# Order of work around the cross-attention maxima in a software-pipelined transformer block

## The chip, the cores and the metric

One core of a Trainium2 chip runs the whole kernel. The metric is the device time of one execution in microseconds (us); lower is better. An execution is one launch of the program, with inputs and outputs in device memory.

## What is computed

32 independent samples of 128 tokens and 128 channels pass one transformer block with 16 heads of width 8: modulated self-attention, cross-attention to a context of 77 tokens, and an MLP with 512 hidden columns. Cut to what matters here:

```
x_norm = modulate(_ln(x), shift_a, scale_a)
q, k, v = split(x_norm @ W_qkv + b_qkv)
attn_out = softmax(q k^T * scale) v @ W_proj + b_proj        # 128 x 128 scores per head
x = x + gate_a * attn_out                                    # called x1 below
q_c = _ln(x) @ W_qc + b_qc
k_c, v_c = split(_ln(context) @ W_kvc + b_kvc)
c_attn_out = softmax(q_c k_c^T * scale) v_c @ W_cproj + b_cproj   # 128 x 77 scores per head
x = x + c_attn_out                                           # called x2 below
x = x + gate_m * (gelu(modulate(_ln(x), ...) @ W_mlp1 + b_mlp1) @ W_mlp2 + b_mlp2)
```

## The kernel before, in words

The 32 samples are worked in 16 pairs. The five engines each run their own instruction stream, written out by hand, and meet through semaphores; every engine takes its stream in order. The attention part is a software pipeline: time is cut into slots, and a slot into 8 beats (t = 0 to 7). In one slot several pairs are at work at once, each in a different phase: `a` (the pair ahead: layer norm and q, k, v), `h` (here: maxima of the self scores, and their exponentials), `d` (one back: end of self-attention, the residual that makes x1, its layer norm, q of the cross-attention, k and v of the context), `f` (two back: the maxima of the cross scores), `e` (three back: cross exponentials and values) and `z` (four back: cross projection and second residual). Slots run from -2 to 19. Slots 0 to 15 have a pair `h`; slots 16 to 19 drain the pipeline and have none. Slot 16 still has `d`, `f`, `e` and `z`; slot 17 has `f`, `e` and `z`. The MLP over 8 groups of 4 samples follows, and its first steps are laid into slots 17 and 18: the first up-projection (`m_up`, L1168) stands at the head of slot 18 on the tensor engine and waits for all maxima of the cross scores.

A softmax needs each row's maximum ahead of the exponential. The tensor engine computes a unit of scores row-wise (`scores`, L1107) into `ps_max`; the vector engine reduces it (`maxima`, L740: `mx` for self, `mxc` for cross). A pair has 4 units u0 to u3, two for each sample. When a sample's two units are done, the pool engine (GpSimd) splits its maxima into two bf16 parts (`split_max`, L565 and L567: `nm`, `nmc`), the tensor engine transposes them (`max_t`, L1222; the job is called max_c0 for the first sample of a cross pair, max_c1 for the second), the scalar engine copies them out (L913) and SyncE's DMA queue writes them as extra rows into the stacked operands (L412). Only then can the transposed scores (`scores_t`, L1118) and the exponentials (L900) of that sample run. The stacked operands themselves (`qk_st`, `qkc_st`) are built by six DMAs for each pair (L407) from parts that the pool engine splits off (`parts`, `high`, `low`; L534, L536, L546, L548). Values are multiplied at L1129. A ring makes units of self and cross scores share `ps_max` in order.

Self units stand in beats 0 to 3, cross units in beats 4 to 7. The small jobs of a beat follow the unit on the tensor engine: the projection (`proj`, L1338 and L1341) in beat 4, k and v of the context (`kv_c`, L1350 and L1354) in beat 5; max_c0, the flipped cross sums (`oc_t`, L1204) and the transposed x1 (`x1_t`, L1196) in beat 6; the q projection of the cross-attention (`q_c`, L1217) and the flipped cross output (`obc_t`, L1204) in beat 7. On the vector engine the residual that makes x1 stands in beat 4 (L757), statistics and their aggregation in beat 5 (L702, L709), the normalisation in beat 6 (L718, writes `x_n`), the division of the cross output (`attention_out`, L747 and L751) at the head of beat 7. The pool engine turns the variance into the reciprocal deviation (`rstd`, L524 and L529). In the trace a digit in a name is left out: x_mv, x_ve, x_rstd and x_n stand for x and for x1 alike; SPq is SyncE's queue of DMA issues.

Of the kernel before, what the change touches and what calls it, by code (L numbers as in the profile page):

```python
# [26 lines left out]
S = 77  # L27
# [156 lines left out]
def block_kernel(nc, x, cond, ctx, w_mod, b_mod, w_qkv, b_qkv, w_proj, b_proj, w_qc, b_qc, w_kvc, b_kvc,  # L184
# [5 lines left out]
    with es:  # L190
# [303 lines left out]
        def _(pool):  # L494
# [65 lines left out]
            def split_max(p, b, mxt, nmt, counted, high, both, taken):  # L560

                if not p.first():
                    w(pool, taken, 2 * p.n + b - 1)
                hold(pool, counted, NU * p.n + 2 * b + 2)
                nc.gpsimd.tensor_copy(nmt[:, b, 0], mxt[:, b]).then_inc(sems[high], 1)  # L565
                w(pool, high, 2 * p.n + b + 1)
                nc.gpsimd.tensor_tensor(nmt[:, b, 1], mxt[:, b], nmt[:, b, 0], ALU.subtract).then_inc(sems[both], 1)  # L567
# [17 lines left out]
            def slot(s):  # L585
                far, a, h, d, f = (s.pair(n) for n in ("far", "ahead", "here", "back1", "back2"))
                if f:
                    parts(f, qcx[:], [qkcp[:, 0, n] for n in range(3)], qcr[:], "qc0_set", "qc", "qkc_in")
                if s.last(2):
                    m_rstd_step(0)  # L590
                if far:
                    rstd("x", far)
                if h:
                    split_max(h, 0, mx, nm, "mx_set", "nmh_set", "nm_set", "mts_ps")
                if d:
                    gated(d)
                if a:
                    high(a, qkx[:], [qkp[:, :, n] for n in range(3)], qkr[:], "qkx_set", "qk", "qk_in")
                if h:
                    split_max(h, 1, mx, nm, "mx_set", "nmh_set", "nm_set", "mts_ps")  # L600
                if a:
                    low(a, [qkp[:, :, n] for n in range(3)], qkr[:], "qk")
                if d:
                    rstd("x1", d)
                if f:
                    split_max(f, 0, mxc, nmc, "mxc_set", "nmch_set", "nmc_set", "mtc_ps")
                if h:
                    rstd("ctx", h)
                if d:
                    parts(d, kcx[:].rearrange("c (b k) -> c b k", b=G), key_parts,  # L610
                          kcr[:].rearrange("c (b k) -> c b k", b=G), "kvc0_set", "kc", "qkc_in")
                if f:
                    split_max(f, 1, mxc, nmc, "mxc_set", "nmch_set", "nmc_set", "mtc_ps")
                if far and far.first():
                    pool.wait_ge(sems["x_n_set"], 1)
                    for par in range(2):
                        nc.gpsimd.memset(qkc_st[par][:, :, 1].bitcast(u32), 0).then_inc(sems["z_pool"], 1)
                    nc.gpsimd.memset(qkcp[:].bitcast(u32), 0).then_inc(sems["pad_set"], 1)
                    pool.wait_ge(sems["z_pool"], 8)
                    for par in range(2):  # L620
                        nc.gpsimd.memset(qkc_st[par][:, :, 1].rearrange("c m (b k) -> c m b k", b=G)[:, :, :, 0:S],
                                         1.0).then_inc(sems["zk_set"], 1)
                if a and a.first():
                    pool.wait_ge(sems["wc_in"], 16 * 2)
                    for n, src in ((2, wqc_sb), (3, wkvc_sb)):
                        for s_ in range(2):
                            last = nc.gpsimd.tensor_copy(
                                wdh[:, n, HALF * s_:HALF * (s_ + 1)].rearrange("c (d m) -> c d m", d=D),
                                src[:, 0:C].rearrange("c (m s d) -> c s d m", s=2, d=D)[:, s_])
                        last.then_inc(sems["wdc_set"], 1)  # L630
# [8 lines left out]
        def _(dve):  # L639
# [72 lines left out]
            def normalise(kind, p, src, taken):  # L712
                L = ln[kind]
                w(dve, f"{kind}_rstd_set", p.n + 1)
                if not p.first():
                    w(dve, taken, p.n)
                for b in range(G):
                    last = nc.vector.tensor_scalar(L["xn"][:, b], src(b), L["mv"][:, b, 0:1], L["rstd"][:, b:b + 1],  # L718
                                                   ALU.subtract, ALU.mult)
                last.then_inc(sems[f"{kind}_n_set"], 1)  # L720
# [7 lines left out]
            def x_of(p):  # L728
                return lambda b: xs[:, batch(p, b)].rearrange("t o c -> t (o c)")
# [63 lines left out]
            def slot(s):  # L793
                far, a, h, d, f, e, z = (s.pair(n) for n in ("far", "ahead", "here", "back1", "back2", "back3", "back4"))
                for t in range(BEATS):

                    if t == 3 and s.last(2):
                        dve.wait_ge(sems["x2_set"], NPAIR - 3)
                        m_norm(0, 0, True)
                    if t == 0 and s.last(1):  # L800
                        m_norm(1, 1)

                    if t == 1 and z:
                        residual(z, "projc_ps", "proj_c", "x2_set")
                    if t == 3 and d:
                        attention_out(d, "s", "o_t", "ot_ps", "rden_set", "o_set", "obt_ps")
                    if t == 7 and e:
                        attention_out(e, "c", "oc_t", "oct_ps", "rdenc_set", "oc_set", "obct_ps")

                    use = s.unit(self_max(t))  # L810
                    if use:
                        maxima(*use, "smax_ps", mx, T, "mx_set", "nm_set")
                    use = s.unit(cross_max(t))
                    if use:
                        maxima(*use, "smaxc_ps", mxc, S, "mxc_set", "nmc_set")

                    if t == 0 and far:
                        arrived("x_in", far, {0: (0,), 1: (1,), 4: (2,), 5: (3, 4)})
                        stats("x", far, x_of(far))
                        aggregate("x", far)  # L820
                        if far.first():
                            tables(range(2), 1)
                            head_columns()
                    if t == 4 and d:
                        residual(d, "proj_ps", "proj", "x1_set")
                    if t == 5 and d:
                        hold(dve, "x1_set", d.n + 1)
                        stats("x1", d, x_of(d))
                        aggregate("x1", d)
                    if t == 1 and h:  # L830
                        arrived("c_in", h, {0: (0,), 1: (1,), 3: (2, 3, 4)})
                        stats("ctx", h, ctx_of(h))
                        aggregate("ctx", h)
                    if t == 5 and far:
                        normalise("x", far, x_of(far), "xt_ps")
                        if far.first():
                            tables(range(2, 6), 2)
                            for st in qkc_st:
                                nc.vector.memset(st[:, :, 0].bitcast(u32), 0).then_inc(sems["zq_set"], 1)
                            for vt in v_m:  # L840
                                nc.vector.memset(vt[:], 0.0).then_inc(sems["z_dve"], 1)
                            key_sums()
                    if t == 6 and d:
                        normalise("x1", d, x_of(d), "x1t_ps")
                    if t == 7 and h:
                        normalise("ctx", h, ctx_of(h), "ctxt_ps")
                if a and a.first():
                    gate_rows()
# [230 lines left out]
        def _(pe):  # L1079
# [107 lines left out]
            def slot(s):  # L1187
# [37 lines left out]
                for t in range(BEATS):  # L1225
                    use = s.unit(self_max(t))
                    if use:
# [2 lines left out]
                        if u == 0:  # L1230
                            w(pe, f"qk_in{p.par}", 16 * NCMB * (p.turn + 1))
                        scores(p, u, qk_st, T, "smax_ps")
                    use = s.unit(cross_max(t))
                    if use:
                        p, u = use
                        ring_free(s, MAX_RING, "cross", u, max_read)
                        if u == 0:
                            w(pe, f"qkc_in{p.par}", 16 * NCMB * (p.turn + 1))
                        scores(p, u, qkc_st, S, "smaxc_ps")
                    use = s.unit(self_exp(t))  # L1240
                    if use:
                        p, u = use
# [123 lines left out]
                        flip_out("obc_t", "c", e, "oc_set", "obct_ps")  # L1366
                    if t == 7 and far:
                        transposed("x_t", "x", far, T, "xt_ps")
                    if h and h.first() and t < 4:
                        spread(4 + t, ps_st[:, t % 2])  # L1370
                if a and a.first():
# [60 lines left out]
```

## Time and profile before

| | us |
|---|---|
| median of 3 runs | 414.25 |
| lowest and highest | 413.67, 418.06 |
| the profiled execution's own time | 416.58 |
| its span, first to last instruction | 414.8 |
| mean granted TensorE clock in it | 0.960 |

The 1.78 us between the profiled execution's time and its span lie outside the instructions. Stretches of the trace are named by us from the start of the span. The self maxima of slot 0 begin at 26.1, of slot 3 at 80.1, of slot 11 at 218.8 and of slot 15 at 286.9; slot 16 begins at 303.4, and the first up-projection of the MLP starts at 336.9.

### The profile page before, as it was taken

What the parts mean: (1) busy time and instruction counts of PE and PEld (TensorE: products, weight loads), DVE (VectorE), ACT (ScalarE), POOL (GpSimd) and SP (SyncE); (2) the same over time, 40 slices, a digit from 0 to 9 for tenths busy, and PEclk for the clock granted to TensorE, in tenths of its full rate; (3) what the DMA queues carried; (4) which work ended last, traced back from release to release, by engine and by line L of the source; (5) the groups of instructions that cost most, each with busy time, mean ns of one, the idle gap of its engine ahead of it and who ended that gap; (6) DMA issues with size and microseconds to landing.
All of it is one profiled execution on the core that took longest, in us unless ns stands there. A gap on an engine that the chain in (4) does not pass through costs nothing.

```text
span 414.8 us, 15984 instructions
## 1 busy us (share of the span) xinstructions
PE 349.4 (84%) x5880; PEld 237.8 (57%) x5880; DVE 254.0 (61%) x650; ACT 268.6 (65%) x523; POOL 216.7 (52%) x494
## 2 busy tenths in 40 slices
PE   3475867889899989999899989998777787999994
PEld 2343545566666766767667667676555454445442
DVE  5653637668777887878877788777635350434311
ACT  1134444668677887878878887787672457577572
POOL 7724357657776676776867668666252310211200
PEclk9999978899999999999999999999997588999998
DMA  5053358251432424325343352343230300000101
GB/s 149 13 138 86 88 155 175 72 143 44 119 91 70 117 70 122 91 70 127 72 106 91 78 136 70 92 100 74 68 80 1 81 4 1 25 27 25 51 25 51
DMA packets 65548, 33.13 MB, mean 80 GB/s; under 512 B 8359, under 2 KB 65255, under 8 KB 65511
## 3 DMA queue, kind: packets, MB, share of 16 engines
q1 hardware_dynamic: 63599, 32.56, 32.1%
q8 instruction: 24, 0.39, 0.4%
q10 hardware_dynamic: 1912, 0.07, 0.3%
q14 instruction: 13, 0.11, 0.1%
HBM read 4.83 MB, written 2.10 MB: 17 GB/s over the span
## 4 chain that ended last, share of the span: by engine, by line
PE 37%; issue 20%; DVE 18%; POOL 11%; SPq 6%; DMA 3%; ACT 2%; ACTq 1%; DVEq 1%; POOLq 1%
DVE mx L740 10%; PE ps_o L1176 7%; PE wide L1168 7%; PE ps_o L1129 5%; SPq L407 5%; PE wide L1107 4%; POOL qkp L536 3%; PE ps_misc L1204 3%; PE ps_misc L1217 3%; PE wide L1118 3%; POOL qkp L534 2%; DMA qk_st<-nmT 2%; PE ps_misc L1196 2%; DVE x_stats L702 1%; DVE ctx_stats L702 1%
## 5 line engine op out<-in xcount | busy, mean ns | idle before, releaser
L740 DVE TENSOR_REDUCE mx<-wide 128x8 f32<-128x1024 f32 x64 | 78.0, 1219 | 27.1 <-PE wide L1107 27.1
L900 ACT ACTIVATE p_c<-wide 128x1024 f32<-128x1024 f32 x64 | 65.5, 1023 | 33.4 <-PE wide L1118 33.0
L900 ACT ACTIVATE p_s<-wide 128x1024 f32<-128x1024 f32 x64 | 65.5, 1024 | 21.5 <-PE wide L1118 21.0
L740 DVE TENSOR_REDUCE mxc<-wide 128x8 f32<-128x616 f32 x64 | 50.8, 794 | 24.7 <-PE wide L1107 24.6
L1129 PE MATMUL ps_o<-p_s,v_m 128*32 128x128 f32 x1024 | 44.5, 294 | 0.6
L1129 PE MATMUL ps_o<-p_c,vc_m 128*32 128x128 f32 x1024 | 44.3, 294 | 0.3 <-ACT s_sum L921 0.2
L524 POOL TENSOR_TENSOR x_ve<-x_mv,eps_sb 128x2 f32<-128x2 f32 x32 | 6.4, 201 | 57.9 <-DVE x_mv L709 57.9
L1118 PE MATMUL wide<-qk_st 64*128 64x128 bf16 x512 | 26.9, 226 | 7.6 <-DMA qk_st<-nmT 5.6
L1107 PE MATMUL wide<-qk_st 62*128 62x128 bf16 x512 | 27.3, 231 | 6.0 <-DVE mx L740 4.5
L1129 PEld LDWEIGHTS ps_o<-p_s,v_m 128*32 128x32 f32 x1024 | 26.1, 114 | 8.7 <-issue 3.5
L1129 PEld LDWEIGHTS ps_o<-p_c,vc_m 128*32 128x32 f32 x1024 | 25.7, 114 | 8.0 <-issue 1.1
L1168 PE MATMUL wide<-m_nT,w_sb 128*128 128x512 f32 x64 | 29.9, 602 | 0.2 <-DVE mxc L740 0.2
L1118 PE MATMUL wide<-qkc_st 64*128 64x128 bf16 x512 | 26.2, 223 | 3.5 <-ACT p_c L900 3.3
L1176 PE MATMUL ps_o<-qk_st,w_sb 128*128 128x512 f32 x64 | 28.9, 594 | 0.0
L1107 PEld LDWEIGHTS wide<-qk_st 62*128 62x128 bf16 x512 | 15.5, 99 | 23.1 <-DVE mx L740 18.7
L1107 PE MATMUL wide<-qkc_st 62*128 62x77 bf16 x512 | 20.5, 203 | 9.7 <-DMA qkc_st<-qkcp 9.3
L571 POOL TENSOR_TENSOR m_ve<-m_mv,eps_sb 128x4 f32<-128x4 f32 x8 | 1.6, 200 | 48.1 <-DVE m_mv L776 48.1
L1107 PEld LDWEIGHTS wide<-qkc_st 62*128 62x128 bf16 x512 | 12.3, 97 | 22.0 <-issue 18.7
L757 DVE TENSOR_TENSOR xs<-xs,ps_misc 128x256 f32 (+1 forms) x32 | 13.5, 421 | 18.3 <-PE ps_misc L1341 11.0
L529 POOL TENSOR_TENSOR x_rstd<-x_ve,mhalf 128x2 f32<-128x2 f32 x32 | 22.4, 700 | 2.9 <-POOL x_ve L524 0.8
L951 ACT ACTIVATE m_y<-ps_o,gb_m,mod 128x128 f32<-128x128 f32 x32 | 12.0, 456 | 18.0 <-PE ps_o L1176 18.0
L790 DVE TENSOR_TENSOR m_out<-xs,ps_misc 128x512 f32<-128x512 f32 x8 | 5.5, 687 | 29.6 <-PE ps_misc L1184 29.6
(154 smaller groups left out, 828.1 us busy)
## 6 DMA issues: line engine op xcount, KB each, us to landing
qk_st<-qkp SPq DMA_DIRECT2D x96, 128.0 KB, 2.6
qkc_st<-qkcp SPq DMA_DIRECT2D x96, 128.0 KB, 2.5
out<-m_out SPq DMA_DIRECT2D x8, 256.0 KB, 2.3
xs<-x SPq DMA_DIRECT2D x3, 512.0 KB, 3.9
qk_st<-nmT SPq DMA_DIRECT2D x64, 4.0 KB
qkc_st<-nmcT SPq DMA_DIRECT2D x64, 4.0 KB
ctx_sb<-ctx SPq DMA_DIRECT2D x3, 308.0 KB
w_sb<-L_xcond_W_mlp SPq DMA_DIRECT2D x2, 256.0 KB, 3.9
```

The lines of the kernel that those rows point to most:

```text
L407: sp.dma_start(dst[c:128:ROWSTEP], parts[:].rearrange("c a p t -> c (a p) t")[:, a:b + 4:b + 3 - a]).then_inc(sems[name], 16)
L529: nc.gpsimd.tensor_tensor(L["rstd"][:], L["ve"][:], mhalf[0:L["rows"], 0:G], ALU.pow).then_inc(sems[f"{kind}_rstd_set"], 1)
L536: nc.gpsimd.tensor_tensor(dst[2], rest, dst[1], ALU.subtract).then_inc(sems[f"{name}2_set"], 1)
L740: nc.vector.reduce_max(mxt[:, b].rearrange("q (x r) -> q r x", r=2)[:, r], src, AX.X, negate=True).then_inc(sems[done], 1)
L757: nc.vector.tensor_tensor(xs[:, batches(p)], xs[:, batches(p)], ps_misc[BANK[job]][:, 0:GT].rearrange("t (b c) -> t b c", b=G), ALU.add).t ...
L900: nc.scalar.activation(dst[u % 2][:].rearrange("k x q -> k (x q)"), ps_st[:].rearrange("k s x -> k (s x)"), ACT.Exp, scale=SCALE).then_inc ...
L1107: last = mm(ps_max[:, s_, j * T:j * T + keys], st[p.par][lo:lo + KROWS, m, 0, b * T:(b + 1) * T], st[p.par][lo:lo + KROWS, m, 1, b * T:b * ...
L1118: last = mm(ps_st[:, s_, j * T:(j + 1) * T], st[p.par][lo:lo + HALF, m, 1, b * T:(b + 1) * T], st[p.par][lo:lo + HALF, m, 0, b * T:(b + 1) ...
L1129: last = mm(ps_o[32 * j:32 * j + 32, at:at + T], vt[p.par][:, b, 4 * j + 2 * r + s_], probs[u % 2][:, 4 * s_ + j], start=(s_ == 0), stop=( ...
L1168: mm(ps_h[k], w1_sb[:, k * 128:(k + 1) * 128], m_nT[par][:], start=True, stop=True).then_inc(sems["m_h_ps"], 1)
L1176: last = mm(ps_y[:, :], w2_sb[:, k], hT[par][:, k], start=(k == 0), stop=(k == NF - 1))
L1204: last = tr(dst[:, n * 128:(n + 1) * 128], src, ident[:])
```

## The change

Three orders change; no instruction is added or taken away.

1. Pool engine, slots with `h`: `split_max(f, 0)` now comes ahead of `rstd("x1", d)`. It has an effect where `d` and `f` exist, in slots 2 to 15.
2. Vector engine, slots without `h` (16 and 17): the maxima of a cross unit come after the residual, the statistics and the normalisation of their beat, and the statistics of x1 move from beat 5 to beat 4. The division of the cross output stays ahead of the maxima in beat 7.
3. Tensor engine, slots without `h`: the row-wise cross scores come last in their beat, after the transposed scores, the values and the small jobs.

```
@@ pool, slot(s)
-                if d:
+                if d and not h:
                     rstd("x1", d)
                 if f:
                     split_max(f, 0, mxc, nmc, "mxc_set", "nmch_set", "nmc_set", "mtc_ps")
+                if d and h:
+                    rstd("x1", d)
@@ vector, slot(s), in the loop over t
                     use = s.unit(cross_max(t))
-                    if use:
+                    if use and h:
                         maxima(*use, "smaxc_ps", mxc, S, "mxc_set", "nmc_set")
...
-                    if t == 5 and d:
+                    if t == (5 if h else 4) and d:
                         hold(dve, "x1_set", d.n + 1)
                         stats("x1", d, x_of(d))
                         aggregate("x1", d)
...
                     if t == 6 and d:
                         normalise("x1", d, x_of(d), "x1t_ps")
+                    if use and not h:
+                        maxima(*use, "smaxc_ps", mxc, S, "mxc_set", "nmc_set")
@@ tensor, slot(s), in the loop over t
-                    use = s.unit(cross_max(t))
-                    if use:
-                        p, u = use
-                        ring_free(s, MAX_RING, "cross", u, max_read)
-                        if u == 0:
-                            w(pe, f"qkc_in{p.par}", 16 * NCMB * (p.turn + 1))
-                        scores(p, u, qkc_st, S, "smaxc_ps")
+                    def rows_max():
+                        ...
+                    if h:
+                        rows_max()
...
                     if t == 7 and far:
                         transposed("x_t", "x", far, T, "xt_ps")
+                    if not h:
+                        rows_max()
```

## Rows read from the trace of the kernel before

**Rows 1.** The page: busy time of each engine.

```profile
PE 349.4 (84%) x5880; PEld 237.8 (57%) x5880; DVE 254.0 (61%) x650; ACT 268.6 (65%) x523; POOL 216.7 (52%) x494
```

**Rows 2.** Timeline of PE, slot 10: start, duration, operands, [idle before <- releaser].

```profile
214.88 0.23 PE L1222 MATMUL ps_misc<-ident,nmc 128*32 128x128 bf16 x1 [0.80 <-POOL nmc L567]
215.53 0.38 PE L1196 MATMUL ps_misc<-ident,x_n 128*128 128x128 f32 x2
215.84 0.31 PE L1107 MATMUL wide<-qkc_st 62*128 62x77 bf16 x8
216.23 0.40 PE L1118 MATMUL wide<-qk_st 64*128 64x128 bf16 x8
```

**Rows 3.** Timelines of POOL and DVE, the same slot.

```profile
213.37 0.21 POOL L524 TENSOR_TENSOR x_ve<-x_mv,eps_sb 128x2 f32<-128x2 f32 x1 [1.69 <-DVE x_mv L709]
214.59 0.23 POOL L567 TENSOR_TENSOR nmc<-mxc,nmc 128x16 bf16<-128x16 f32 x1
...
211.71 0.79 DVE L740 TENSOR_REDUCE mxc<-wide 128x8 f32<-128x616 f32 x1
214.41 0.59 DVE L718 TENSOR_SCALAR x_n<-xs,x_mv,x_rstd 128x128 f32 x2
```

**Rows 4.** Timeline of SyncE's DMA issues, the same slot.

```profile
213.86 1.15 SPq L412 DMA_DIRECT2D qk_st<-nmT  x2
```

**Rows 5.** The chain that ended last, in order of time, slot 14.

```profile
282.88 1.63 DMA qk_st<-nmT
...
284.65 0.40 PE wide L1118 x8
```

**Rows 6.** Timelines of PE and of SyncE's issues, slot 3.

```profile
95.52 0.38 PE L1196 MATMUL ps_misc<-ident,x_n 128*128 128x128 f32 x2
95.84 0.32 PE L1107 MATMUL wide<-qkc_st 62*128 62x77 bf16 x8
95.99 0.39 PE L1118 MATMUL wide<-qk_st 64*128 64x128 bf16 x8
...
92.07 1.14 SPq L412 DMA_DIRECT2D qk_st<-nmT  x2
```

**Rows 7.** Timelines of PE, DVE and SyncE's issues, slot 15.

```profile
301.18 0.38 PE L1196 MATMUL ps_misc<-ident,x_n 128*128 128x128 f32 x2
...
299.97 0.60 DVE L718 TENSOR_SCALAR x_n<-xs,x_mv,x_rstd 128x128 f32<-128x128 f32 x2 [0.25 <-POOL x_rstd L529]
...
293.21 4.79 SPq L412 DMA_DIRECT2D qk_st<-nmT  x4
```

**Rows 8.** Timelines of PE and POOL, slot 16.

```profile
312.71 0.32 PE L1107 MATMUL wide<-qkc_st 62*128 62x77 bf16 x8 [2.75 <-DMA qkc_st<-qkcp]
318.63 0.22 PE L1222 MATMUL ps_misc<-ident,nmc 128*32 128x128 bf16 x1 [0.94 <-POOL nmc L567]
320.56 1.22 PE L1217 MATMUL ps_misc<-x1T,wdh 128*128 128x256 f32 x2 [0.38 <-ACT nmcT L913]
...
322.44 0.40 POOL L546 CAST qkcp<-qcx 128x256 bf16<-128x256 f32 x1 [0.73 <-issue]
```

**Rows 9.** Timelines of PE and DVE, slot 17 and the head of 18.

```profile
329.93 0.44 PE L1107 MATMUL wide<-qkc_st 62*128 62x77 bf16 x8 [0.85 <-DMA qkc_st<-qkcp]
332.12 1.08 PE L1129 MATMUL ps_o<-p_c,vc_m 128*32 128x128 f32 x16
333.13 1.12 PE L1158 MATMUL ps_misc<-ident,m_n 128*128 128x128 f32 x4
336.93 1.12 PE L1168 MATMUL wide<-m_nT,w_sb 128*128 128x512 f32 x2 [0.20 <-DVE mxc L740]
...
335.74 0.42 DVE L751 TENSOR_TENSOR c_o<-ps_misc,c_rden 128x256 f32<-128x256 f32 x1
```

**Rows 10.** Stretches of 6 us: engines' busy time, TensorE clock (PEclk), DMA.

```profile
312.00:318.00 6.00, 4.98 (x108) 3.79 (x108) 2.88 (x8) 2.12 (x4) 0.86 (x3) 0.72 0.00 0
...
324.00:330.00 6.00, 3.88 (x63) 2.28 (x62) 2.69 (x13) 3.07 (x3) 2.04 (x4) 0.50 0.55 133
```

More of the change, by code:

```diff
@@ L1232, in slot @@
                         scores(p, u, qk_st, T, "smax_ps")
-                    use = s.unit(cross_max(t))
-                    if use:
-                        p, u = use
-                        ring_free(s, MAX_RING, "cross", u, max_read)
-                        if u == 0:
-                            w(pe, f"qkc_in{p.par}", 16 * NCMB * (p.turn + 1))
-                        scores(p, u, qkc_st, S, "smaxc_ps")
+                    def rows_max():
+                        use = s.unit(cross_max(t))
+                        if use:
+                            p, u = use
+                            ring_free(s, MAX_RING, "cross", u, max_read)
+                            if u == 0:
+                                w(pe, f"qkc_in{p.par}", 16 * NCMB * (p.turn + 1))
+                            scores(p, u, qkc_st, S, "smaxc_ps")
+                    if h:
+                        rows_max()
                     use = s.unit(self_exp(t))
```

## The prediction, as recorded before the changed kernel was seen

> **What bounds the kernel now.** The page first: PE is the busiest engine at 84%, the others lie between 52% and 65% [rows 1]. That is too little for a bound by work alone, so the question is which waits lie on the path. I read three stretches: a slot of the loop, the two slots where a wait differs from the loop's, and the drain. Each is read on the timeline of PE first, then on the engine that released it.
>
> In a slot of the loop PE has one visible stall: 0.80 us ahead of max_c0, released by POOL's nmc [rows 2]. POOL had been idle 1.69 us, waiting for the mean and variance of x1, while the maxima that it was to split next were ready at 211.71 + 0.79 = 212.50 [rows 3]. The first edit goes for exactly this stall. But 1 us later PE meets a second gate that is easy to miss, for it stands between two groups that look adjacent. The row-wise cross scores start at 215.84 and the transposed self scores of unit 2 at 216.23, 0.39 us apart [rows 2]; in slot 3 the same two groups are 95.99 - 95.84 = 0.15 us apart [rows 6]. The missing 0.24 us are a wait for the DMA that writes the second sample's self maxima: it is issued as a pair at 213.86 and 1.15 us long [rows 4], and the chain of slot 14 shows that the second of a pair lands 1.63 us after its own start and PE starts 0.14 us after that [rows 5]. So 213.86 + 0.59 (half of the pair and the gap) + 1.63 + 0.14 = 216.22, and PE started at 216.23. In the timelines the distance from this pair's issue to those scores is 2.35 to 2.38 us in slot 2 and in slots 4 to 14, 12 slots with the same number: PE waits for the DMA in all of them.
>
> **Part 1, the split ahead of the deviation (slots 2 to 15).** POOL splits in its idle time: two instructions of about 0.2 us, 0.5 us with their gap, from 212.6 to 213.1. The mean and variance arrive for the instruction at 213.37 [rows 3], so the deviation isn't pushed back. Max_c0 leaves the path: it can run at about 213.9, when the values ahead of it are issued. What is late next is x1_t: it needs x_n, which ends at 214.41 + 0.59 = 215.00 [rows 3], and so starts at 215.05 to 215.15 where it now starts at 215.53 [rows 2]. At best that is 0.4 us for PE. Then comes the gate. The DMA pair hangs on POOL's parts of q and k and on the five stack DMAs that stand ahead of it in SyncE's queue and are issued back to back, all of it ahead of the edit and fed by the self maxima of beats 0 to 3, which follow the slot's start on PE. None of it moves. PE will wait about 0.6 us at the transposed scores where it now waits 0.24, and everything after them, the q projection and the next slot's first rows included, stays where it is. Gain in 12 slots: 0. Also moved are POOL's deviation of the context, the parts of the context's k and the first max DMA of the cross pair, each about 0.4 us earlier; nobody on the path waits for them.
>
> In two slots the gate is open. In slot 3 the pair was issued at 92.07 and landed by 92.07 + 0.59 + 1.63 = 94.3, while the scores ran at 95.99 [rows 6]; x1_t goes from 95.52 to about 95.1: 0.4 us, and slot 4 begins that much earlier with all that feeds its DMAs. In slot 15 the last of four issues ends at 293.21 + 4.79 = 298.00 and has landed by 299.1, long before x1_t at 301.18; x_n ends at 299.97 + 0.60 = 300.57 [rows 7], so x1_t can start at 300.7: 0.45 us. The lower bound of part 1 is therefore -0.85 us for both, the upper is 0 if either is eaten by a later DMA.
>
> **Part 2, slot 16.** PE stands 2.75 us at the cross rows of unit 0, for a DMA [rows 8], and behind this wait are queued the transposed scores of unit 3, the values and the projection. With the new order these run inside the stall: x1 is summed about 3 us earlier and its statistics are done at about 312.6. But the loop through the maxima is long. From the DMA (312.71 less the 0.4 won in slot 15, 312.3): rows 0.3, values and kv_c 2.2 (1.4 at full clock), rows 0.3, maxima 0.8, split 0.6, max_c0, oc_t and x1_t 1.3 to 1.7, copy 0.4. That puts q_c at 317.7 to 318.9 where it is 320.56 now [rows 8]. This gain isn't passed on whole. POOL's stream has the split of the second sample ahead of the parts of q_c; it waits for the maxima of unit 3, whose rows now stand on PE behind q_c and obc_t; obc_t waits for the division on DVE, and that stands behind the maxima of unit 2. So from x1_t: rows 0.3, maxima 0.8, division 0.9, obc_t 0.35, rows 0.3, maxima 0.8, split 0.5 = 4 us, a chain that now overlaps with q_c. POOL's first part of q_c, at 322.44 now [rows 8], comes at 321.2 (clock full) to 322.8 (clock halved). PEclk was 0.72 in this stretch [rows 10]; I take 321.8, 0.6 us earlier, the 0.45 of slot 15 in it.
>
> **Part 2, slot 17.** Its rows of unit 0 wait for the DMA that follows from POOL's parts, so they come 0.6 us earlier too. From them to the first up-projection it is now 336.93 - 329.93 = 7.0 us [rows 9], because the row scores run ahead of the jobs. In the new order each unit stands behind its beat's jobs: rows 0.4, values 1.1, m_transpose 1.1, rows 0.35, maxima 0.8, split 0.6, max_c0 and oc_t 0.8, rows 0.35, maxima 0.85, division 0.9, obc_t 0.35, rows 0.35, maxima 0.85 = 8.8 to 8.9 us. (Values, m_transpose and division by [rows 9], maxima and split by [rows 3].) What is moved ahead of the DMA (one unit of scores and of values) was off this chain before, too, once the ring of maxima is counted. So slot 17 costs 1.9 us, and no cover hides it: the up-projection is queued on PE ahead of max_c1, the projection and the last four exponentials, and DVE's next normalisation stands behind the same maxima.
>
> **Sum.** Slot 3 -0.4, slots 15 and 16 -0.6, slot 17 +1.9: +0.9 us. On the profiled execution's own time 416.58 + 0.9 = 417.5. That execution was 2.3 us over the median, so I put the sum on the median: 414.25 + 0.9 = 415.1. The runs shown spread by 4.4 us, which alone is 1%; a change of under 1%, 4.1 us, is what this kernel's times can't well tell from none.
>
> **Rivals.**
>
> A. The clock. After the 2.75 us stall PEclk is 0.72 from 312 to 318, and 0.50 from 324 to 330 [rows 10], against a mean of 0.96 over the span: at half clock 16 value products take 1.08 us [rows 9], where they take 0.64 in the loop. The new order breaks the long stall into pieces of 1 to 1.5 us. If the clock then stays full through slots 16 and 17, q_c's chain gives 1.9 us instead of 0.6, and slot 17's two groups on PE (2.2 us) halve nearly, while exponentials no longer wait for values at half clock: -0.4 - 1.9 + 1.9 - 1.2 = -1.6 to -2, 412.5 us. For it: the idle time is better spread. Against: the waits on POOL and DVE are new stalls of their own, and with the clock at 0.50 PE was busy 3.88 of 6 us.
>
> The Trainium skill speaks for this rival: "TensorE: Matmul & The Clock Gate" (HAM oscillation — how this bites in real kernels) says that long idle waits of the engine cost it the full clock and that tighter work keeps it. The trace agrees as to the fall after the stall at 312; whether shorter stalls are harmless no row shows.
>
> B. Part 1 is worth its 0.4 us in every slot, because the DMA pair moves with the rest: 14 x 0.4 = 5.6 less and 0.2 less in slot 16, 1.9 more in slot 17: 414.25 - 3.9 = 410.4 us. Against it stands the same 2.36 us in 12 slots.
>
> C. Slower: the new order of slots 16 and 17 lets PE idle more often, the clock falls earlier and comes back later than 334. Then slot 16 gives nothing (+0.4), slot 17 costs 2.3, and slot 18 runs at half clock: its four groups of values and two first up-projections cost 0.44 us more each (1.08 against 0.64), 2.6 us. 414.25 - 0.4 + 0.4 + 2.3 + 2.6 = 419.2 us. It decides if q_c comes later than 321.
>
> D. The reordering of slots 16 and 17 does nothing, as what is won ahead of the DMA is what is lost behind it: 413.4 to 414.3 us.
>
> **Chances.** Forecast (414.3 to 417.5) 0.50, D 0.15, A 0.17, B 0.07, C 0.08, the rest 0.03. The range of 8 in 10 takes in the forecast, D and most of A, and the spread of the runs: 411.8 to 417.8. Faster by over 1% (under 410.1) 0.07; slower by over 1% (over 418.4) 0.08; within 0.85.
>
> **What would show it.** Right: max_c0 has no idle time ahead of it in slots 2 to 15; x1_t starts 0.4 us sooner against the transposed scores of unit 2, which still start 2.36 us after the issue of the DMA pair; the slots of the loop still take 17.0 us. In slot 16 the projection runs ahead of the DMA's landing; in slot 17 the distance from rows u0 to the up-projection is near 9 us. Wrong: slots of 16.7 us in the loop (B), or PEclk of 1.00 from 318 to 330 (A). The forecast fails if the DMA pair's issue hangs on something that the early split also frees, or if the drain's clock differs from that of before.

## The result and the profile after

| | before, beside it | after |
|---|---|---|
| median of 4 runs, us | 416.15 | 420.41 |
| lowest and highest | 413.67, 418.13 | 419.17, 422.58 |
| the profiled execution's own time | 416.58 | 419.17 |
| its span | 414.8 | 417.4 |
| mean granted TensorE clock in it | 0.960 | 0.957 |

After over before is 1.0111 (interval 1.0066 to 1.0156): slower by 1.1%. The forecast was 415.1, range 411.8 to 417.8, with 0.85 on "within 1%". All ratios here and below leave out, as a slower state, executions that took over 1.5% longer than the fastest of their kernel; medians take in all.

Three places of the changed kernel answer to the rows of before. First a loop slot, in the timelines of PE, of SyncE's issues, of POOL and of DVE, the slot of [rows 2] to [rows 4]:

```profile
213.03 0.22 PE L1226 MATMUL ps_misc<-ident,nmc 128*32 128x128 bf16 x1
...
214.31 0.41 PE L1200 MATMUL ps_misc<-ident,x_n 128*128 128x128 f32 x2 [0.48 <-DVE x_n L720]
214.66 0.31 PE L1111 MATMUL wide<-qkc_st 62*128 62x77 bf16 x8
215.24 0.40 PE L1122 MATMUL wide<-qk_st 64*128 64x128 bf16 x8 [0.27 <-DMA qk_st<-nmT]
...
212.88 1.14 SPq L412 DMA_DIRECT2D qk_st<-nmT  x2
...
212.11 0.22 POOL L567 TENSOR_TENSOR nmc<-mxc,nmc 128x16 bf16<-128x16 f32 x1
212.54 0.21 POOL L524 TENSOR_TENSOR x_ve<-x_mv,eps_sb 128x2 f32<-128x2 f32 x1 [0.21 <-DVE x_mv L711]
...
200.71 1.22 DVE L742 TENSOR_REDUCE mx<-wide 128x8 f32<-128x1024 f32 x1 [1.20 <-PE wide L1111]
217.77 1.23 DVE L742 TENSOR_REDUCE mx<-wide 128x8 f32<-128x1024 f32 x1 [1.26 <-PE wide L1111]
```

Max_c0 no longer waits (of slots 2 to 15 only in slot 14, 0.32 us). X1_t now has the visible stall, 0.48 us, and the transposed scores have the other one, which this time the trace names: 0.27 us, for the DMA of the pair. They start 215.24 - 212.88 = 2.36 us after the issue of the pair, as before (216.23 - 213.86 = 2.37, [rows 2, 4]). The slot takes 217.77 - 200.71 = 17.06 us; the mean of the four slots 10 to 13 is 17.0 in both kernels. One wait went, the gate behind it stood, and the loop gained nothing.

Second, the drain on PE, and POOL's part of q_c; these answer to [rows 8] and [rows 9]:

```profile
311.12 0.32 PE L1111 MATMUL wide<-qkc_st 62*128 62x77 bf16 x8 [0.92 <-DMA qkc_st<-qkcp]
314.61 0.22 PE L1226 MATMUL ps_misc<-ident,nmc 128*32 128x128 bf16 x1 [1.67 <-POOL nmc L567]
316.25 0.70 PE L1221 MATMUL ps_misc<-x1T,wdh 128*128 128x256 f32 x2 [0.37 <-ACT nmcT L917]
...
327.50 1.08 PE L1133 MATMUL ps_o<-p_c,vc_m 128*32 128x128 f32 x16
328.51 0.44 PE L1111 MATMUL wide<-qkc_st 62*128 62x77 bf16 x8
...
332.76 0.22 PE L1226 MATMUL ps_misc<-ident,nmc 128*32 128x128 bf16 x1 [1.66 <-POOL nmc L567]
335.62 0.66 PE L1208 MATMUL ps_misc<-ident,c_o 128*128 128x128 f32 x2 [1.81 <-DVE c_o L753]
337.58 2.07 PE L1172 MATMUL wide<-m_nT,w_sb 128*128 128x512 f32 x2 [0.92 <-DVE mxc L742]
...
320.19 0.40 POOL L546 CAST qkcp<-qcx 128x256 bf16<-128x256 f32 x1
```

The 2.75 us stall of slot 16 is 0.92 now, though 1.67 us for POOL's split have come behind it, and q_c comes at 316.25 instead of 320.56. In slot 17 PE has three long waits: 1.66, 1.81 and 0.92 us, for POOL's split, for DVE's division and for the last maxima. Before, max_c0 had none there, and the last maxima cost 0.20 [rows 9]. The division cost 0.58:

```profile
334.42 0.23 PE L1222 MATMUL ps_misc<-ident,nmc 128*32 128x128 bf16 x1
...
336.32 0.41 PE L1204 MATMUL ps_misc<-ident,c_o 128*128 128x128 f32 x2 [0.58 <-DVE c_o L751]
```

From its first rows to the first up-projection it is 337.58 - 328.51 = 9.1 us, where it was 7.0 [rows 9]. The up-projection's line has a second message in its duration: its first two matmuls take 2.07 us where the same two took 1.12 [rows 9]. They are the same instructions at half clock. Third, therefore, stretches of after (us, then busy time of PE, PEld, DVE, ACT, POOL, then PEclk, DMA):

```profile
312.00:318.00 6.00, 3.23 (x49) 2.09 (x39) 3.21 (x7) 2.25 (x6) 2.65 (x8) 0.91 0.02 3
...
330.00:337.00 7.00, 3.19 (x35) 2.04 (x35) 2.56 (x5) 2.75 (x7) 0.41 (x2) 0.74 0.01 1
337.00:346.00 9.00, 7.25 (x85) 3.55 (x85) 3.25 (x14) 4.31 (x8) 1.62 (x4) 0.79 0.01 4
...
330.50:334.00 3.50, 1.66 (x24) 0.99 (x22) 0.91 (x2) 1.90 (x6) 0.41 (x2) 0.99 0.00 0
334.00:340.80 6.80, 4.25 (x33) 1.96 (x33) 3.76 (x14) 0.65 (x2) 1.62 (x4) 0.50 0.01 2
```

and of before, for 330 to 337 and 337 to 346, which the prediction does not show:

```profile
330.00:337.00 7.00, 6.04 (x84) 3.86 (x84) 3.93 (x8) 3.49 (x8) 0.41 (x2) 0.71 0.01 2
337.00:346.00 9.00, 7.27 (x109) 3.80 (x109) 2.59 (x13) 5.90 (x10) 1.62 (x4) 0.91 0.02 5
```

From 330 to 337 PE is busy 3.19 of 7 us, where it was 6.04. Before, the half clock of the drain ends in that stretch and slot 18 begins at full clock. After, the clock is full again already at 330.5, PE is busy 1.66 of the next 3.5 us, with the first of the three waits among them, and from 334.0 to 340.8 the clock is at half. So slot 18 begins at half clock, and from 337 to 346 PE runs 85 matmuls where it ran 109.

In what follows three distances of each profile stand beside the times: the period of a loop slot (a quarter of the time from the first self maxima of slot 10 to those of slot 14), slot 17 (from DVE's first cross maxima of the slot to the first up-projection), and the tail (from there to the end of the span). Before: 16.99, 6.51, 77.85. After: 17.00, 8.56, 79.79. So slot 17 is 2.05 us longer and what follows 1.94. Each distance is that of one profiled execution.

### The profile page after: what moved, and what is told of

The parts are those of the page before. It is cut to its first block and busy times, and to the rows that moved or that the text cites. A ratio compares the mean times of both kernels' runs of the same rounds, so it can differ in the third digit from the quotient of the medians.

```text
span 417.4 us, 15984 instructions
## 1 busy us (share of the span) xinstructions
PE 349.0 (84%) x5880; PEld 236.4 (57%) x5880; DVE 254.7 (61%) x650; ACT 269.1 (64%) x523; POOL 216.8 (52%) x494
## 5 line engine op out<-in xcount | busy, mean ns | idle before, releaser
L1133 PE MATMUL ps_o<-p_c,vc_m 128*32 128x128 f32 x1024 | 43.4, 290 | 0.8 <-ACT p_c L904 0.6
L1172 PE MATMUL wide<-m_nT,w_sb 128*128 128x512 f32 x64 | 31.5, 629 | 0.9 <-DVE mxc L742 0.9
L1122 PEld LDWEIGHTS wide<-qk_st 64*128 64x128 bf16 x512 | 17.2, 99 | 15.1 <-issue 12.0
L565 POOL CAST nmc<-mxc 128x16 bf16<-128x16 f32 x32 | 6.3, 195 | 35.4 <-issue 23.6
L1200 PE MATMUL ps_misc<-ident,x_n 128*128 128x128 f32 x64 | 14.0, 304 | 11.9 <-DVE x_n L720 11.8
```

Of the source, the lines that this page charges most:

```text
L1122: last = mm(ps_st[:, s_, j * T:(j + 1) * T], st[p.par][lo:lo + HALF, m, 1, b * T:(b + 1) * T], st[p.par][lo:lo + HALF, m, 0, b * T:(b + 1) ...
L1133: last = mm(ps_o[32 * j:32 * j + 32, at:at + T], vt[p.par][:, b, 4 * j + 2 * r + s_], probs[u % 2][:, 4 * s_ + j], start=(s_ == 0), stop=( ...
L1172: mm(ps_h[k], w1_sb[:, k * 128:(k + 1) * 128], m_nT[par][:], start=True, stop=True).then_inc(sems["m_h_ps"], 1)
L1200: last = tr(dst[:, b * rows:(b + 1) * rows], ln[kind]["xn"][:, b], ident[0:rows, 0:rows])
```

## The experiments

Ratios are to the kernel before, side by side, with the 95% interval, from 6 or 12 runs of the kernel and 23 or 29 of before. The medians of before beside them were 416.28 (e1 to e4), 417.26 (e5 to e8), 416.51 (e9 to e12) and 416.52 (e13 to e16).

**Which part costs: e1 to e4.** e1 has the pool engine's order alone; e2 has the new order of DVE and PE in slots 16 and 17 alone; e3 that in slot 16 alone, e4 in slot 17 alone.

```
 e1:  POOL hunk of the change only
 e2:  DVE and PE hunks only (POOL as before)
 e3:  -if use and h:        +if use and not s.last(3):     # s.last(3): slot 16
      -if not h: rows_max() +if s.last(3): rows_max()      # and so on, POOL as before
 e4:  the same with s.last(2)                              # slot 17
```

> Part 1 alone: only the pool engine's order changes, in slots 2 to 15. Gate theory (the DMA pair of the second sample's self maxima holds the transposed scores of unit 2 in 12 slots): the loop keeps its 17.0 us for a slot, max_c0 loses its stall, the distance from the pair's issue to those scores stays 2.36 us, and the whole is 0.5 to 1.5 us faster than before (what the trace of the changed kernel already shows up to slot 15: self maxima of slot 15 at 285.4 instead of 286.9). Rival (the early split itself costs time in executions that weren't profiled): 1 to 4 us slower. Rival (the gain adds up in every slot): 4 us or more faster.

> Parts 2 and 3 alone: the vector and tensor engines' order in slots 16 and 17, the pool engine's as before. If the drain is where the loss comes from: slower than before by what the whole change costs and what part 1 gives, 4 to 6 us, with rows u0 of slot 17 to the first up-projection at 9 us instead of 7.0. If the loss comes from the split: within 1 us of before.

> Only slot 16 has the new order on the vector and tensor engines; slot 17 and the pool engine are as before. Theory: slot 16 gains about 1 us (the pool engine's parts of the q projection come 1 us earlier, as in the changed kernel) and nothing in slot 17 gives it back: 0.5 to 1.5 us faster than before. Rival (both slots' orders are bad, because each breaks the tensor engine's work into more stalls and the clock falls): slower by 1 to 3 us.

> Only slot 17 has the new order. Theory: its chain from the rows of unit 0 to the first up-projection takes 9 us instead of 7.0, +2 us, and the first up-projection and slot 18 run at half clock for a further 1 to 2 us: 3 to 5 us slower than before. Rival (slot 17's loss is hidden by other work of slot 18): under 1 us.

| | ratio | median | slot | slot 17 | tail |
|---|---|---|---|---|---|
| e1 | 0.9995 (0.9962 to 1.0029) | 416.25 | 17.00 | 6.50 | 77.86 |
| e2 | 1.0109 (1.0071 to 1.0146) | 419.60 | 17.00 | 8.22 | 80.21 |
| e3 | 1.0004 (0.9963 to 1.0045) | 415.74 | 16.99 | 6.06 | 77.67 |
| e4 | 1.0106 (1.0054 to 1.0158) | 420.53 | 16.99 | 8.28 | 80.17 |

The whole loss is slot 17's. The split and slot 16, each expected to gain 0.5 to 1.5 us by itself, are worth nothing that can be measured. PE in e4 (timeline):

```profile
332.88 0.22 PE L1224 MATMUL ps_misc<-ident,nmc 128*32 128x128 bf16 x1 [1.67 <-POOL nmc L567]
...
335.97 0.66 PE L1206 MATMUL ps_misc<-ident,c_o 128*128 128x128 f32 x2 [1.81 <-DVE c_o L751]
...
337.93 2.08 PE L1170 MATMUL wide<-m_nT,w_sb 128*128 128x512 f32 x2 [0.92 <-DVE mxc L740]
```

The same three waits and the same up-projection at half clock as in the changed kernel, without the other two parts.

**Whether the DMA pair is the loop's gate: e5 and e6.** e5 moves the issue of the pair ahead of the last two of the five stack DMAs; e6 adds the split of part 1. If the pair is the gate, the slot gets shorter now, and the split, worth nothing by itself, gets a value.

```
 if a: w qk1_set; stack(..., 1)
+if h: w nmT_set; max_rows(qk_st[h.par], 1, nmT, ...)
 if a: w qk2_set; stack(..., 2)
-if h: w nmT_set; max_rows(qk_st[h.par], 1, nmT, ...)
```

> The kernel before, with one edit on SyncE's queue: the DMA pair of the second sample's self maxima is issued after three of the five stack DMAs instead of after all five. Gate theory: the pair can go when the scalar engine has copied the maxima out, about 1.3 us earlier, and no longer holds the transposed scores of unit 2; the stall at max_c0 is then the only one, and PE gains the 0.24 us that it now waits at those scores: 0.2 us in each of 12 slots, 2 to 3 us in all. Rival (the slot is set by the vector engine or by PE and the wait is incidental): no change, or up to 1 us slower since two stack DMAs go 1.2 us later.

> The same edit of SyncE's queue together with part 1, the early split. Gate theory: with the gate open the 0.4 us that the early split wins on PE before x1_t reach the next slot: 0.24 + 0.4 = 0.6 us in each of 12 to 13 slots, 7 us or 1.8% faster than before, slots of 16.4 us instead of 17.0. Rival (another gate stands right behind, such as the vector engine's chain of self maxima or the stack DMAs of the next pair): no more than the run without the split gives.

| | ratio | median | slot | slot 17 | tail |
|---|---|---|---|---|---|
| e5 | 0.9946 (0.9912 to 0.9981) | 414.18 | 16.80 | 6.55 | 77.84 |
| e6 | 0.9898 (0.9843 to 0.9953) | 412.39 | 16.50 | 6.97 | 77.65 |

Timelines of PE, SyncE's issues and DVE in e6, the slot of [rows 2]:

```profile
208.87 0.41 PE L1199 MATMUL ps_misc<-ident,x_n 128*128 128x128 f32 x2 [0.48 <-DVE x_n L721]
209.22 0.31 PE L1110 MATMUL wide<-qkc_st 62*128 62x77 bf16 x8
209.36 0.39 PE L1121 MATMUL wide<-qk_st 64*128 64x128 bf16 x8
...
204.18 1.94 SPq L407 DMA_DIRECT2D qk_st<-qkp  x3
206.25 1.15 SPq L412 DMA_DIRECT2D qk_st<-nmT  x2
...
211.89 1.23 DVE L743 TENSOR_REDUCE mx<-wide 128x8 f32<-128x1024 f32 x1 [0.82 <-PE wide L1110]
228.46 1.23 DVE L743 TENSOR_REDUCE mx<-wide 128x8 f32<-128x1024 f32 x1 [0.77 <-PE wide L1110]
```

The pair is issued at 206.25 behind three DMAs, 3.11 us ahead of the scores, which now follow the rows by 0.14 us: the wait is gone. A slot is 0.5 us shorter with the split and 0.2 without it, so behind the open gate the split is worth 0.3 us a slot; behind the closed one it was worth 0.00. Both fell short of what the two visible pieces had promised (0.24 for the gate, 0.4 for the split), and e6 gained 1.0% in all where 1.8% was expected. The next wait, x_n's 0.48 us, stands there already; that it holds the slot now was not tested.

**Whether the clock is the second half of slot 17's loss: e7, e8, e9.** These put matmuls whose result nobody reads into the stalls: 128x48 each, into columns of PSUM that nobody reads before they are written again (of `ps_st` in e7 and e9, of `ps_max` in e8). They leave out nothing of the computation. e7 and e9 are e4 with them ahead of max_c0, of obc_t and of the first up-projection: 14, 14 and 8 in e7, 28, 28 and 14 in e9. e8 is the kernel before with 28 ahead of the first cross rows of slot 16 and 8 in slot 17.

```
+def fill(n):
+    for i in range(n):
+        mm(ps_st[:, i % 2, (i//2 % 4)*T + 80 : (i//2 % 4)*T + 128], ones[:], ones[:, 0:48], ...)
+if t == 6 and s.last(2): fill(14)   # e9: 28     ahead of max_c0
+if t == 7 and s.last(2): fill(14)   # e9: 28     ahead of obc_t
+if t == 0: fill(8)                  # e9: 14     slot 18, ahead of m_up
```

> The new order in slot 17 alone, as in the run before it, plus idle matmuls on PE that write a part of PSUM that nobody reads: 14 ahead of max_c0, 14 ahead of obc_t (slot 17), 8 ahead of the first up-projection, each set sized to lie inside the stall that is there. Clock theory (2 us of the 4.5 are half clock in slot 18, which follows PE's stalls in slot 17): the clock is full from the first up-projection on, the distance from it to the end falls from 80.2 to about 78 us, and the kernel is 2 to 3 us faster than without the fill, some 2 us slower than before. Rival (the loss lies in the order of the waits alone): no gain, or slower by the length of the fill, 0 to 2 us.

> The kernel before plus idle matmuls on PE inside its stall for the DMA at the first cross rows: 28 in slot 16, 8 in slot 17. Clock theory: PEclk stays at 1.00 after the stall of 2.75 us, the value products of slot 17 take 0.64 us instead of 1.08, and the run is 1 to 3 us faster than before. Rival (the later, shorter stalls bring the clock down all the same, or the drain is bound by DMAs and not by PE): within 0.5 us of before.

> As the filled run of slot 17, with twice as many idle matmuls (28, 28 and 14), since 14 took only 0.52 us of stalls of 1.7 us and the first up-projection still ran at half clock. Clock theory: PE is busy through slot 17, the first up-projection takes 1.1 us instead of 2.1, its distance to the end is 78 us, and the kernel comes to 0 to 2 us over before. Rival (the clock isn't what the fill changes): no better than the run with 14, or worse by the added work, 1 to 2 us.

| | ratio | median | slot 17 | tail |
|---|---|---|---|---|
| e7 | 1.0043 (1.0011 to 1.0076) | 419.65 | 7.76 | 79.68 |
| e8 | 0.9965 (0.9930 to 1.0000) | 416.23 | 6.71 | 78.02 |
| e9 | 1.0067 (1.0022 to 1.0112) | 418.05 | 8.49 | 77.66 |

In the profile of e7 the clock is not back, against what was expected: the fills took 0.37 to 0.52 us of each wait, and the up-projection still runs at half.

```profile
330.52 0.52 PE L1191 MATMUL wide<-ones 128*128 128x48 bf16 x14
...
336.69 2.08 PE L1170 MATMUL wide<-m_nT,w_sb 128*128 128x512 f32 x2 [0.62 <-DVE mxc L740]
```

In that of e9 it is back (timeline of PE, and two stretches with the columns of [rows 10]):

```profile
331.25 1.19 PE L1191 MATMUL wide<-ones 128*128 128x48 bf16 x28
...
333.97 0.87 PE L1191 MATMUL wide<-ones 128*128 128x48 bf16 x28
335.84 0.41 PE L1211 MATMUL ps_misc<-ident,c_o 128*128 128x128 f32 x2 [1.00 <-DVE c_o L751]
...
337.42 1.13 PE L1170 MATMUL wide<-m_nT,w_sb 128*128 128x512 f32 x2 [0.47 <-DVE mxc L740]
...
330.00:337.00 7.00, 5.40 (x105) 4.15 (x105) 2.72 (x5) 2.72 (x7) 0.42 (x2) 0.85 0.01 1
337.00:346.00 9.00, 6.70 (x109) 3.55 (x109) 3.09 (x14) 5.47 (x9) 1.63 (x4) 1.00 0.01 4
```

PE is busy 5.40 of 7 us (3.19 in the changed kernel, 3.53 in e4), the next stretch has a clock of 1.00 (0.79 and 0.63), the up-projection takes 1.13, and the tail is 77.66 where e4 has 80.17: 2.5 us. Slot 17 is still 8.49. So one profile shows the two halves apart: the fill takes away the tail's part and leaves the chain's. The times say the same with less force: the ratios of e7 and e9 lie under e4's 1.0106, with intervals that overlap its own. E8, the kernel before with fills, has an interval that ends at 1.0000: the fill has no large price of its own. Its clock did not do what was expected, though. It fell to half again behind later waits, and the values of slot 17 took 1.08 us as before:

```profile
315.74 0.22 PE L1227 MATMUL ps_misc<-ident,nmc 128*32 128x128 bf16 x1 [1.89 <-POOL nmc L567]
...
329.04 1.08 PE L1129 MATMUL ps_o<-p_c,vc_m 128*32 128x128 f32 x16
```

The Trainium skill says in "TensorE: Matmul & The Clock Gate" (HAM oscillation — how this bites in real kernels) that long idle waits of the engine cost it the full clock. The runs agree, and add that waits of 0.9 to 1.8 us close together were enough here (1.66, 1.81 and 0.92 in the changed kernel, with the clock at 0.50 from 334.0), with no longer one among them.

**What each beat of slot 17 costs: e10, e13, e14.** The new order in beats 4 and 5 alone (s.last(2) and t < 6), in beat 6 alone, in beat 7 alone.

> Slot 17 has the new order in beats 4 and 5 alone; in beats 6 and 7 the rows stand ahead of max_c0, oc_t and obc_t again. Theory (the chain is lengthened where rows stand behind a job that itself waits: max_c0 for the pool engine in beat 6, obc_t for the vector engine's division in beat 7): nearly all of the loss is gone, rows u0 to the first up-projection at 7.0 to 7.6 us, the kernel within 1 us of before. Rival (the values and m_transpose ahead of the rows of units 0 and 1 are what costs): 2 us or more slower than before.

> Slot 17 has the new order in beat 6 alone: the rows of unit 2 stand behind max_c0 and oc_t, so behind the pool engine's split. Theory: they move from right after the maxima of unit 1 to 1.5 us later, and the first up-projection with them: 1.3 to 2 us slower than before, a third to a half of slot 17's cost. Rival (beat 7 carries all): within 0.5 us of before.

> Slot 17 has the new order in beat 7 alone: the rows of unit 3 stand behind obc_t, so behind the vector engine's division. Theory: 1.2 to 2 us slower than before. Rival (beat 6 carries all, beat 7's division comes ahead of these maxima on the vector engine anyway): within 0.5 us of before.

| | ratio | median | slot 17 | tail | first up-projection, us |
|---|---|---|---|---|---|
| e10, beats 4, 5 | 1.0021 (0.9975 to 1.0067) | 417.33 | 5.51 | 79.05 | 2.08 |
| e13, beat 6 | 1.0039 (0.9995 to 1.0082) | 419.26 | 7.03 | 79.69 | 2.08 |
| e14, beat 7 | 1.0063 (1.0027 to 1.0098) | 419.52 | 7.98 | 79.90 | 1.63 |

Beats 4 and 5 cost little or nothing. Their rows come later, which makes the distance of e10 short, since it starts with them; slot 17 and tail together are 84.56 us, and 84.36 in before. Beats 6 and 7, where the rows of units 2 and 3 now stand behind a job that itself waits (max_c0 for POOL's split, obc_t for DVE's division), carry the loss: 0.4% and 0.6%. That the two add up to e4's 1.06% isn't shown: e13's interval reaches below 1, and in the profiles slot 17 and tail together are 2.4 us (e13), 3.5 (e14) and 4.1 (e4) longer than before's. In e10 the profile shows the first up-projection at half clock as well, in a kernel that the times don't call slower:

```profile
331.42 0.31 PE L1109 MATMUL wide<-qkc_st 62*128 62x77 bf16 x8 [0.93 <-DVE mxc L740]
...
334.64 2.08 PE L1170 MATMUL wide<-m_nT,w_sb 128*128 128x512 f32 x2
```

One profile is one execution; where the clock comes back within slots 17 and 18 isn't the same in each.

**The same pair again, side by side: e15 and e16.** e15 is the kernel of e4, e16 that of e9.

> The new order in slot 17 alone, once more, as the partner of the next run. By the first time: 1.06% slower than before.

> The same with 28, 28 and 14 idle matmuls in PE's stalls. Clock theory: 1.5 to 2.5 us (0.4 to 0.6%) faster than its partner, and its profile has the first up-projection at 1.1 us where the partner's has 2.1. Rival: no faster than the partner.

| | ratio | median | slot 17 | tail |
|---|---|---|---|---|
| e15 | 1.0104 (1.0054 to 1.0154) | 420.65 | 8.22 | 80.25 |
| e16 | 1.0011 (0.9966 to 1.0056) | 419.12 | 8.35 | 79.95 |

The intervals meet only at their ends: by the ratios the fill takes back 0.9%, by the medians 1.5 us or 0.4%. But the profile of e16 misses its expectation. Its first up-projection took 1.78 us, between what it takes at either level, and the tail 79.95. PE had been busy 5.14 of the 7 us ahead, nearly as in e9, and the clock fell all the same:

```profile
337.50 1.78 PE L1170 MATMUL wide<-m_nT,w_sb 128*128 128x512 f32 x2 [0.47 <-DVE mxc L740]
...
330.00:337.00 7.00, 5.14 (x109) 3.93 (x105) 2.65 (x5) 2.75 (x7) 0.41 (x2) 0.93 0.01 4
337.00:346.00 9.00, 7.29 (x87) 3.56 (x85) 3.16 (x14) 4.47 (x8) 1.62 (x4) 0.81 0.02 4
```

Three fills gave 1.0043, 1.0067 and 1.0011, by the medians 1.0057, 1.0037 and 1.0062. All lie under the two without, 1.0106 and 1.0104, by the medians 1.0102 and 1.0099. That filling the stalls wins time is shown; whether it is 0.4% or 0.9% isn't.

**The best of both: e11 and e12.** e11 is the early pair, the split and the new order in slot 16 alone; slot 17 is as before. e12 adds 16 idle matmuls (into `ps_max`) ahead of the first cross rows of slots 16 and 17.

```
 e11 = after, with  h  ->  not s.last(3)  in the DVE and PE hunks, and e5's SyncE edit
 e12 = e11 + fill(16) at t == 4 of slots 16 and 17, ahead of rows_max()
```

> The early DMA pair, the early split and the new order in slot 16 alone; slot 17 as before. If slot 16's gain adds to the other two: 1 us under the run with pair and split, ratio 0.985 to 0.99 to before. Rival (slot 16's order gives nothing, as alone): 0.99.

> The run before plus idle matmuls in two waits for DMAs, 16 ahead of the first cross rows in slot 16 and 16 in slot 17. If a fuller clock in the drain is worth having: 1 to 2 us under that run. Rival (the pieces of stall that stay bring the clock down anyway, as in the fill of the kernel before): the same as that run.

| | ratio | median | slot | slot 17 | tail | span |
|---|---|---|---|---|---|---|
| e11 | 0.9853 (0.9784 to 0.9921) | 408.26 | 16.47 | 6.51 | 77.84 | 406.5 |
| e12 | 0.9846 (0.9779 to 0.9912) | 407.29 | 16.48 | 5.82 | 78.52 | 403.4 |

Both are 1.5% faster than before (2.0% and 2.2% by the medians), and e11 comes to 0.9853 / 1.0111 = 0.975 of the changed kernel, an estimate from runs that were not side by side. The fill of e12 adds nothing that can be told from e11, and e11's interval overlaps e6's.

**All 18 profiles together.** The tail goes with the mean granted clock of the 12 us from the first up-projection on:

| clock | tail | profiles |
|---|---|---|
| 1.00 | 77.65 to 77.67 | e3, e6, e9 |
| 0.86 | 77.84 to 78.02 | before, e1, e5, e8, e11 |
| 0.88, 0.89 | 79.05, 78.52 | e10, e12 |
| 0.76 to 0.80 | 79.68 to 80.25 | after, e2, e4, e7, e13 to e16 |

E9 has slot 17's new order and e3 and e6 the old one, and their tails are equal: what the tail loses is the clock's and not the order's. The half clock of before comes at 344.4, 7.5 us behind the up-projection, and costs 0.2 us. E10 and e12 have a short slot 17; with it they come to 84.56 and 84.34, before to 84.36. And the order does bring the clock down: in all 8 profiles with the old order in slot 17 the first up-projection takes 1.12 or 1.13 us, in all 7 with the new one in whole or in part and no fill it takes 1.63 to 2.08.

## Why the prediction was wrong

**The loop: right.** "Gain in 12 slots: 0": the period is 17.00 in e1 and after, the distance from the pair's issue to the scores 2.36 us, and the ratio of e1 0.9995. e5 and e6 show it from the other side: with the pair issued earlier the period falls to 16.80, and to 16.50 with the split. Rival B's 0.4 us a slot need the pair to come earlier with the rest; where it does (e6) the split is worth 0.3.

**Slots 3 and 15, the gains of 0.4 and 0.45: not resolved.** From the self maxima of slot 3 to those of slot 4 it is 18.46 us before and 17.38 after, but e3, e4, e13 and e14, whose streams there are those of before, have 19.60, 18.03, 18.09 and 18.51. The pipeline's fill varies by more than the term. In slot 3 the pair's issue itself moved to 92.92, where it had been 92.07 [rows 6], and the transposed scores ran 2.36 us after it: in that execution the gate had closed there too. In slot 15 it was open, as forecast (the transposed scores 0.15 us behind the rows), but x1_t ran 14.55 us behind the slot's first self maxima, where it ran 14.31 before; in kernels with the streams of before it is 14.4 to 16.0.

**Slot 16, "0.6 us earlier": q_c's gain came, what reached slot 17 can't be told.** Counted from slot 15's first self maxima, q_c starts after 30.4 to 32.3 us in the five profiles with the new order in slot 16 and after 32.9 to 35.5 in the other 13. (The terms of the working add up to 317.4 to 318.6 for q_c, 0.3 less than it says; this changes nothing.) POOL's first part of q_c comes after 34.3 to 36.3 and 34.8 to 37.4, the first maxima of slot 17 after 42.5 to 44.4 and 42.9 to 45.6: the scatter is wider than the 0.6 us, and e3's ratio of 1.0004 (0.9963 to 1.0045) can't tell 0.6 us from none. One step is wrong by the trace: "Its rows of unit 0 wait for the DMA". After, the last of the stack DMAs has landed at 327.5, and the rows start at 328.51 without a wait, right behind the values that the new order put ahead of them, 1.08 us at half clock. Before, they started 0.13 us behind the landing. That eats 0.9 us there.

**Slot 17, the step that failed.** The prediction put it at "1.9 us, and no cover hides it". The chain is right to 0.2 us: 2.05 us in after, 1.71 and 1.77 in e2 and e4. But the term was taken as the whole price, and e4 alone costs 1.06%, 4.4 us on 416.3. The rest is the tail, 77.85 to 80.17: slot 18 begins at half clock, a term that the sum put at nothing. The working had listed all the waits that make up the 8.9 us, on POOL's split, DVE's division and the last maxima, and hadn't asked what they do to PE: they are idle time of PE, 1.66 + 1.81 + 0.92 = 4.4 us within the 6.5 from 331.1 to the up-projection.

**Rival C had this, and 0.08.** It named slot 18 at half clock and priced it at 2.6 us; measured are 1.9 (after) to 2.4 (e15). Its total of 419.2 against 414.25 is +4.9; measured is 1.1%, +4.6. The text gives no reason against it, and the reason that it gives against rival A ("new stalls of their own") speaks for it. Besides, [rows 9] showed the first up-projection at 1.12 us, full clock, after a slot at half: the clock had come back just in time there, with PE busy 6.04 of 7 us, and the new order took half of that. Its condition ("if q_c comes later than 321") was wrong: q_c came at 316.25, and the clock fell all the same, in slot 17. Its 2.6 us are right in sum and partly by luck: it took 0.44 us more for each of two up-projections, while the first took 0.95 more (2.07 for 1.12) and the second ran at full clock.

**Rival A** was half seen: after the shorter first stall of slot 16 the clock is 0.91 from 312 to 318, where it was 0.72 [rows 10]. It was 0.50 again from 318 to 330.

**The base.** The forecast was put on 414.25, the median of three runs. Beside the experiments before's medians were 416.3 to 417.3, so some 2 us of the 5.3 by which 415.1 missed 420.41 are the base and not the change. The profiled execution, which the text called 2.3 us over the median, was nearer to the truth.

## What to carry to other kernels

When a visible stall is taken away, look for a pair of groups that stand further apart than the same pair elsewhere: a constant distance from a DMA's issue to its reader is the gate, and moving that issue can be worth more than the stall (here 0.2 us a slot against 0.0, and 0.5 for both). When an order is chosen for a drain, count the waits that the new order puts on TensorE twice, once on the chain and once for the clock of what runs next. Put the longest dependent chain (scores, maximum, split, transpose) first in its beat wherever the slot is bound by it, as slot 17 is here, and fill the wait with the jobs rather than the reverse.

## What the runs showed of the hardware

Matmuls that do nothing useful can pay: 70 of them in the waits of slot 17 brought a slower kernel from 1.0104 to 1.0011 of before, side by side; by the medians, from 420.65 to 419.12 us. Of the two profiles with these 70, one kept the full clock into slot 18 and the other did not.

Kernels with the same instructions up to slot 3 started that slot between 77.6 and 80.1 us, while the loop behind it repeated to 0.01 us. The clock does not explain it: up to 77.6 us it was 0.80 in e9, which started slot 3 at 77.7, and 0.96 in before, which started it at 80.1. What it is stays open. Differences under 1% needed a stretch of the profile with its own two ends; the span didn't tell them.
